# Second stage's convolution: three batches of the third chunk on Pool, none of it on VectorE, five on TensorE

## The reference

```python
def _L0_attn_ref(x, ln_w, ln_b, A_log, B_mat, C_mat, D_vec, out_w, out_b, ...):
    xn = layer_norm(x, ln_w, ln_b)
    A = jax.nn.sigmoid(A_log)
    # h = A*h + B*x_t ;  y_t = sum_n C*h + D*x_t, from h = 0
    y = ssm_scan(xn, A, B_mat, C_mat, D_vec)
    y = jax.nn.silu(y)
    y = linear(y, out_w, out_b)
    x1 = res + y
    ...
```

## Time and profile before

| what | us |
|---|---|
| median of 3 runs | 3006.52 (3006.23 to 3009.16) |
| the profiled execution | 3007.62 |
| its span, first to last instruction | 3005.7 |
| TensorE busy | 2785.7 |
| VectorE busy | 1232.9 |
| ScalarE busy | 987.7 |
| Pool busy | 287.2 |

### The profile page before, as it was taken

How to read it: one execution, slowest core, us unless ns; L and a number is a source line. 1 busy time by engine, 2 the same in 40 slices (tenths; PEclk the granted TensorE clock), 3 DMA queues, 4 the chain that set the end, 5 groups by cost and what they waited for, 6 DMA issues and landing times.

```text
span 3005.7 us, 40740 instructions
## 1 busy us (share of the span) xinstructions
PE 2785.7 (93%) x17928; PEld 1966.6 (65%) x17928; DVE 1232.9 (41%) x1873; ACT 987.7 (33%) x1484; POOL 287.2 (10%) x278
## 2 busy tenths in 40 slices
PE   8979999998899799999999969999999999988698
PEld 3347346456587478888888838778778878853433
DVE  4364343447731633333333342442443343344612
ACT  3243113125342344344334412432332332331210
POOL 1110110221012000000000011011011001000000
PEclk9999999998899999999999979999999999999799
DMA  8964994951021132222222210100100100013198
GB/s 358 356 235 151 377 355 174 382 187 52 15 98 56 57 113 99 98 98 98 98 98 94 92 70 22 42 18 34 47 26 22 47 26 22 26 64 126 43 396 359
DMA packets 61967, 385.52 MB, mean 128 GB/s; under 512 B 6192, under 2 KB 10544, under 8 KB 32352
## 3 DMA queue, kind: packets, MB, share of 16 engines
q1 hardware_dynamic: 27072, 190.58, 16.7%
q0 software_dynamic: 29776, 188.15, 16.3%
q10 hardware_dynamic: 4944, 4.20, 0.4%
HBM read 377.64 MB, written 5.26 MB: 127 GB/s over the span
## 4 chain that ended last, share of the span: by engine, by line
PE 77%; DVE 8%; DMA 3%; ACT 3%; issue 1%; POOL 1%; ACTq 0%; DVEq 0%; POOLq 0%
PE PS L431 11%; PE PS L432 11%; PE PS L433 11%; PE PS L310 4%; PE PS L1859 3%; PE PS L1840 3%; PE PS L631 3%; PE PS L1823 3%; PE PS L1842 3%; PE PS L1841 3%; PE PS L1824 3%; PE PS L1825 3%; PE PS L1876 3%; PE PS L604 2%; DMA PR<-in_ctxN 2%; DVE T L1329 2%
## 5 line engine op out<-in xcount | busy, mean ns | idle before, releaser
L431 PE MATMUL PS<-X_high,W_high 128*128 128x512 f32 x576 | 226.5, 393 | 11.0 <-DVE X_low L1240 11.0
L431 PE MATMUL PS<-H_high,W_high 128*128 128x512 f32 x576 | 224.8, 390 | 2.1 <-DVE rstd L1545 2.1
L432 PE MATMUL PS<-X_low,W_high 128*128 128x512 f32 x576 | 225.8, 392 | 0.0
L433 PE MATMUL PS<-X_high,W_part 128*128 128x512 f32 x576 | 225.5, 392 | 0.0
L432 PE MATMUL PS<-H_low,W_high 128*128 128x512 f32 x576 | 224.8, 390 | 0.0
L433 PE MATMUL PS<-H_high,W_part 128*128 128x512 f32 x576 | 224.6, 390 | 0.0
L1187 DVE TENSOR_TENSOR W_part<-ring,W_high 128x2048 fp32r<-128x2048 f32 x63 | 147.1, 2334 | 185.0 <-ACT W_high L1183 185.0
L1183 ACT ACTIVATE W_high<-ring 128x2048 fp32r<-128x2048 f32 x72 | 137.0, 1914 | 252.4 <-PE PS L433 252.4
L2025 DVE TENSOR_TENSOR RB<-PS,rows 128x512 f32<-128x512 f32 x104 | 71.9, 691 | 312.8 <-PE PS L1842 312.8
L1226 DVE TENSOR_TENSOR H_low<-T,H_high 128x512 fp32r<-128x512 f32 x144 | 99.4, 691 | 210.5 <-ACT H_high L1213 210.5
L1955 ACT ACTIVATE RC<-PS,vec 128x384 f32<-128x384 f32 (+2 forms) x128 | 76.3, 596 | 322.4 <-PE PS L1825 322.4
(11 more groups left out here) (380 smaller groups left out, 5490.5 us busy)
## 6 DMA issues: line engine op xcount, KB each, us to landing
ring<-in_experts SPq DMA_DIRECT2D x83, 1024.0 KB, 4.8
ring<-in_tiles SPq DMA_DIRECT2D x39, 1024.0 KB, 4.9
RC<-in_ctxN POOLq DMA_DIRECT2D x24, 1536.0 KB, 12.3
RA<-in_ctxT POOLq DMA_DIRECT2D x20, 1536.0 KB, 7.2
T<-in_ctxN POOLq DMA_DIRECT2D x24, 1024.0 KB, 16.2
RA<-in_ctxT POOLq DMA_DIRECT2D x12, 1666.0 KB, 14.1
RB<-in_ctxT POOLq DMA_DIRECT2D x12, 1666.0 KB, 15.6
RB<-in_ctxT POOLq DMA_DIRECT2D x12, 1536.0 KB, 10.6
```

The source lines that it names most:

```text
L431: pe.matmul(ps, a, xh, start=start, stop=False)
L432: pe.matmul(ps, a, xl, start=False, stop=False)
L433: return pe.matmul(ps, b, xh, start=False, stop=stop)
```

## The change

Batches 0 to 2 of chunk 2 go to Pool. It waits for the normalisation, multiplies for lag 0, and then for each of the 63 other lags makes a product into one of two small buffers (in a part of RB that holds nothing else then) and adds it to y, three batches of 64 - j tokens. The addition waits for the product; the product waits for what was finished before the last addition. VectorE has chunks 0 and 1 alone, and its wait, written as a count of its shares, now reaches back to the second last instruction. TensorE takes batches 3 to 7 of chunk 2 instead of 1 to 7, and chunk 3 as before. ScalarE waits for both VectorE and Pool ahead of the three silus in place, the last of which is 192 columns wide instead of 64.

```diff
@@ -896,8 +896,8 @@
         CONV_DVE = 2
         CONV_PE = range(CONV_DVE, KC)
-        SHARED = 1
-        dve_shares = [(c, 0, B) for c in range(CONV_DVE)] + [(CONV_DVE, 0, SHARED)]
+        SHARED = 3
+        dve_shares = [(0, 0, B), (1, 0, B)]
         pe_from = {c: SHARED if c == CONV_DVE else 0 for c in CONV_PE}
@@ -1257,6 +1257,16 @@
             for j in range(1, S):
                 pool.wait_ge(*at.own())
                 pool.tensor_tensor(pw[:, j], pw[:, j - 1], abc[:, 0], ALU.mult).then_inc(*at.step("s2.powers"))
+            pool.wait_ge(*at.done("s2.ln1.done"))
+            c, b1 = CONV_DVE, SHARED
+            term = [RB[:, DIAGS * LAGS * P + k * b1 * S:DIAGS * LAGS * P + (k + 1) * b1 * S].rearrange("p (b s) -> p b s", b=b1) for k in (0, 1)]
+            pool.tensor_scalar(y[:, c, 0:b1, :], xn[:, c, 0:b1, :], kconv[:, c, 0:1], None, ALU.mult).then_inc(*at.step())
+            for j in range(1, S):
+                if j > 2:
+                    pool.wait_ge(sems["pool_done"], at.count["pool_done"] - 1)
+                pool.tensor_scalar(term[j % 2][:, :, j:S], xn[:, c, 0:b1, 0:S - j], kconv[:, c, j:j + 1], None, ALU.mult).then_inc(*at.step())
+                pool.wait_ge(*at.own())
+                pool.tensor_tensor(y[:, c, 0:b1, j:S], y[:, c, 0:b1, j:S], term[j % 2][:, :, j:S], ALU.add).then_inc(*at.step("s2.conv.pool"))
             expert_low(pool, at, FFN, 0)
@@ -1298,7 +1308,8 @@
             act.wait_ge(*at.done("s2.conv"))
-            for c, b0, b1 in dve_shares:
+            act.wait_ge(*at.done("s2.conv.pool"))
+            for c, b0, b1 in ((0, 0, B), (1, 0, B), (CONV_DVE, 0, SHARED)):
                 act.activation(Y2[:, c, b0 * S:b1 * S], Y2[:, c, b0 * S:b1 * S], ACT.Silu).then_inc(*at.step("s2.silu"))
```

## The result

The changed kernel takes 3020.83 us (median of 4 runs, 3020.16 to 3023.5), the kernel before 3007.84 in the 4 runs beside them: ratio 1.0045, 95% interval 1.0027 to 1.0062. It is slower by 13 us; the forecast was 3016.3, also slower. The profiled execution took 3023.5 us, its span is 3021.7.

What follows compares the result with a forecast made beforehand. VectorE was taken to end the convolution stage, TensorE 2 us behind. Contended lags 57.2 us plus tail 12.5 moved the end +9.4; with 0.1 for the activations and 0.3 for the clock, +9.8: 3016.3 us, range 3005 to 3030.

Steps and rivals of the forecast that it cites:

- VectorE was the end, TensorE 2 us ahead of it: Convolution stage before the change: VectorE's 189 gapless instructions end it at 786.37 us; TensorE's last lag is out at 784.24.
- the rival without contention: VectorE and Pool don't slow each other in the convolution; the projection starts 7 us earlier, 2999.5 us; chance 10%.
- VectorE's rest is 50 us, the wait's shorter reach free: VectorE's convolution share: 63 narrow instructions go, 10.2 us; alone it would end at 776.0; the shorter wait costs nothing.
- TensorE's forecast of 6.3 us less: TensorE's third chunk falls from 7 to 5 batches, 6.3 us less, so it would be through at about 778.
- Pool alone, 47 us: Pool's convolution lags without contention: 29.0 us of turns and scalars plus 18.1 of elements, done at about 773.
- Contention, one for one while VectorE's instructions are long: Lags 63 to 20: VectorE and Pool alternate, each waiting for the other's data; 57.2 us, with 2.9 hidden.
- The tail, Pool alone for the narrow lags: Lags 19 to 1 of the convolution: Pool sets the pace at 0.66 us each, 12.5 us.
- The end of the stage: Convolution's end moves from 786.37 to 795.8 us, +9.4 us, with Pool last and VectorE a little before.
- the 0.3 us for the lower clock: At the projection, TensorE may stay at the lower clock level a little longer after idling some 17 us: 0.3 us added.
- The upper bound: Convolution's latest end, 813 us, +27: nothing hidden, product at 2.16 ns an element, 0.08 us for its scalar.
- the forecast case: Contention between VectorE and Pool in the convolution makes the kernel slower by +6 to +15 us; chance 53%.
- the rival with expensive products: Contention plus dear Pool products, Pool ending far behind VectorE: +15 to +27 us, 3021 to 3033; chance 20%.

## Why the prediction was right, and where its sum was off

The steps, in its own order:

- **VectorE was the end, TensorE 2 us ahead of it.** Right. With Pool's lags left out TensorE is last, the stage is 8.2 us shorter than before, and the ratio of 0.9963 is 11 us; the rival without contention had 7.
- **VectorE's rest is 50 us, the wait's shorter reach free.** Right, 50.1. TensorE's forecast of 6.3 us less was 6.1 to 6.8 (52.7 beside Pool and VectorE, 52.0 to 52.2 without contention, for 58.9).
- **Pool alone, 47 us.** Wrong, and the largest error: 63.2. The term is the product. From the rows with sums in PSUM, 771 ns at 189 elements and a mean of 536 at a mean of 96, it is 2.5 ns an element and 293 ns fixed, where I had taken 0.83 and 186 + 40 from the one-input cast and put 2.16 as the upper end. The bound was too low, not only the choice. Beside its data it took 0.385 us to the dependent addition (in the changed kernel's narrow tail), where I had 0.26 and 0.04. Of the 16 us, the elements are about 8, the fixed parts 6, and the product for lag 0, which the sum left out, 1. The addition, which had rows, came out as priced: 589 ns at 189 elements and 391 on average, 2.1 ns an element and 187 fixed.
- **Contention, one for one while VectorE's instructions are long.** The mechanism was right, as the run with PSUM shows. Its price was too high: I added 23 us to Pool's 47, it was 14 on 63. Pool's element time in the stretch where both ran is about 24 us (the lags from 63 down to about 18, at 4.37 ns an element for the two), and VectorE lost 15. If elements are what it waited for, some 9 of the 24 lay beside the fixed parts of its instructions, where I had let 2.9 of 18 hide; the traces don't show where they lay. That Pool loses no less with a third of the elements (the run with one batch) is not in the sum at all.
- **The tail, Pool alone for the narrow lags.** Right in kind. I had VectorE a little ahead of Pool; it was ahead by 11.7 us. Down to lags of about 45 tokens the two went through their lags side by side, and from there VectorE drew ahead, where I had put 20. That the dearer product is the reason is likely and not shown by itself.
- **The end of the stage.** Forecast +9.4, in the profiled execution +16.4. The two errors, +16 for Pool alone and -9 for contention, leave +7. TensorE's wait before the projection grew to 26.1 us, not 17. The silus cost 0.1 us more, as summed; the 0.3 us for the lower clock lie inside the scatter of that stretch (29.5 to 30.9 us), so no run shows them.
- **The upper bound.** Its parts, added up as they stand there (2.9 for nothing hidden, 8.0 for the dearer product, 2.5 for its scalar), give 809 and +23, not 813 and +27.

The rule of the Trainium skill, "SBUF — State Buffer", section "Who interferes with whom", that a VectorE instruction with two SBUF inputs contends with a Pool instruction that reads SBUF, holds here for a scalar_tensor_tensor: 65.0 us against 50.1, and 49.4 with one input in PSUM. The Trainium skill says in the same page, section "SBUF: two separate sides", that whoever starts first keeps the shared ports for the whole instruction. Taken for the durations in the trace, that doesn't come out: Pool's lags from 63 down to 18 are by themselves about 50 us (46 x 0.552, and 24 for the elements), and VectorE lost 15 to them.

The measured 3020.83 lies at the upper end of the forecast case (+6 to +15) and by mechanism it is the rival with expensive products, Pool ending far behind VectorE. That the number stayed near the forecast is in part luck: with the 63.2 us that Pool takes alone and the 23 us of contention that I had put on top, the same sum gives by estimate 3032, above the range.

## What to carry to other kernels

Before work is moved from VectorE to Pool, ask whether VectorE's instructions have two inputs in SBUF; if they do, the moved work comes back as waiting on both, and an accumulator in a free PSUM bank ended that here, for 0.5 us more on the two opening products. Price each Pool instruction by a row of its own form: a one-input cast says nothing about a product with a per-partition scalar. Short pairs of dependent instructions are dear on Pool: 0.55 us of each pair here was not data, with two batches as with three.

## What was not expected of the hardware

- Pool's multiplication by a per-partition scalar is dearer than its two-input product with the same coefficient spread by step 0: at 189 elements 771 ns against 494, on average 536 against 348 (sums in PSUM in both).
- An accumulator in PSUM makes VectorE's scalar_tensor_tensor no slower, 738 ns at 504 elements against 739; 126 of them take 49.4 us and not 50.1. The opening tensor_scalar into PSUM takes 746 ns instead of 481 at 512 elements, two of them in all.
- Contention is uneven: with one batch on Pool, VectorE lost 3.3 us over its 126 instructions, and Pool by estimate 17 over its 127; a product of 63 elements took 1.33 us for 0.46 alone.
- A VectorE product with one input and the output in SBUF held Pool's first product up (1259 ns for 789), while a sum with one input in SBUF, one in PSUM and the output in SBUF did not (407 ns for 407).
